# A cross-attention and mixture-of-experts block on one core: ScalarE's exp ahead of its v copies, LN1 one step earlier, the sum over z one step earlier, the high part of z on ScalarE

## The reference

```
q = layernorm(x) @ Wq.T;  k = ctx @ Wk.T;  v = ctx @ Wv.T      # 16 heads of 8
scores = (q . k) / sqrt(8), causal
x = x + (softmax(scores) @ v) @ Wo.T
z = layernorm(x)
rw = softmax(z.mean(over the batch's tokens) @ Wr + br)         # 8 experts
the two best, weights renormalised by a softmax over them
h_e = gelu(z @ W1[e] + b1[e]);  out = sum of the two: w_e * (h_e @ W2[e] + b2[e])
y = out + z;  x = x + layernorm(y) * gamma + beta
```

## Time and profile before

| what | value |
|---|---|
| time, median of 3 runs | 625.79 us (624.58 to 625.92) |
| the profiled execution | 625.34 us, span 623.6 us |
| TensorE matmul, busy share of the span | 88% |
| TensorE weight loads | 62% |
| VectorE | 84% |
| ScalarE | 78% |
| GpSimd | 75% |
| granted TensorE clock, mean | 0.976 |

### The profile page before, as it was taken

The page is one execution under the profiler, slowest core; times in us unless marked ns, Lnnn a source line. Parts: engine busy times, 40 slices in busy tenths (PEclk is TensorE's granted clock), DMA queues, the critical chain, the costliest instruction groups (busy, mean ns, idle before and its releaser), DMA issues.

```text
span 623.6 us, 18950 instructions
## 1 busy us (share of the span) xinstructions
PE 550.3 (88%) x4481; PEld 385.7 (62%) x4481; DVE 521.8 (84%) x1473; ACT 485.9 (78%) x1124; POOL 464.7 (75%) x815
## 2 busy tenths in 40 slices
PE   3899999999999999999999716999999999999782
PEld 2455655556556556555565514788888788888662
DVE  2889898898989898989989756888888888898676
ACT  3677888888787878888887725988888888898494
POOL 5788999999999999999999754755555655554355
PEclk9999999999999999999999967999999999999998
DMA  3010100010010101000020002123322332222135
GB/s 103 27 35 11 35 25 20 22 32 27 8 34 25 34 8 34 25 24 18 17 76 2 2 1 75 56 59 89 98 63 63 89 93 59 85 73 64 44 101 169
DMA packets 55585, 30.03 MB, mean 48 GB/s; under 512 B 4857, under 2 KB 54529, under 8 KB 55553
## 3 DMA queue, kind: packets, MB, share of 16 engines
q1 hardware_dynamic: 55120, 29.47, 16.0%
q10 hardware_dynamic: 432, 0.20, 0.1%
HBM read 13.00 MB, written 4.19 MB: 28 GB/s over the span
## 4 chain that ended last, share of the span: by engine, by line
PE 56%; ACT 14%; DVE 12%; issue 11%; POOL 2%; DVEq 2%; ACTq 2%; DMA 0%; POOLq 0%
PE bank_pair L365 6%; PE scores_banks L354 6%; ACT v_blocks L540 5%; PE scores_banks L484 5%; PE bank_pair L497 5%; PE scores_banks L486 5%; PE scores_banks L485 5%; PE bank_pair L499 5%; PE bank_pair L498 5%; PE bank_pair L378 4%; ACT probs L591 3%; PE bank L328 2%; ACT xn L564 2%; DVE gelu L953 2%; PE bank L390 2%
## 5 line engine op out<-in xcount | busy, mean ns | idle before, releaser
L1072 POOL TENSOR_TENSOR probs<-probs,row_sum_recip 128x512 f32<-128x512 f32 x128 | 133.7, 1045 | 14.7 <-DVE row_sum_recip L792 12.5
L591 ACT ACTIVATE probs<-scores_shifted 128x512 f32<-128x512 f32 x128 | 80.8, 631 | 51.3 <-DVE scores_shifted L786 49.9
L683 ACT ACTIVATE gelu<-scores_banks,b_expert 128x512 f32<-128x512 f32 x144 | 98.5, 690 | 26.3 <-PE scores_banks L486 19.5
L1121 POOL CAST gathered<-z_hi_lo (+1 forms) x114 | 45.9, 438 | 88.7 <-PE scores_banks L486 78.6
L779 DVE TENSOR_REDUCE row_sum<-probs 128x8 f32<-128x512 f32 x128 | 87.1, 680 | 28.7 <-ACT probs L591 28.7
L776 DVE TENSOR_REDUCE row_max<-scores_banks 128x8 f32<-128x512 f32 x128 | 86.9, 679 | 9.1 <-PE scores_banks L354 8.4
L354 PE MATMUL scores_banks<-k_by_head,qT 32*64 32x256 f32 x1024 | 85.0, 401 | 10.3 <-POOL k_by_head L1040 10.2
L902 DVE SCALAR_TENSOR_TENSOR zT_then_yT<-bank_pair,slot_weight,zT_then_yT x288 | 74.7, 282 | 16.9 <-issue 15.5
L786 DVE TENSOR_TENSOR scores_shifted<-scores_banks,row_max 128x512 f32<-128x512 f32 x128 | 86.6, 677 | 0.0
L600 ACT ACTIVATE probsT<-bank_pair 128x512 f32<-128x512 f32 x128 | 76.0, 594 | 13.4 <-PE bank_pair L365 12.6
L365 PE MATMUL bank_pair<-ident,probs 128*128 128x128 f32 x512 | 83.9, 286 | 0.3 <-POOL probs L1072 0.2
(11 more groups left out here) (168 smaller groups left out, 1162.6 us busy)
## 6 DMA issues: line engine op xcount, KB each, us to landing
gathered<-z_hi_lo SPq DMA_DIRECT2D x187, 64.0 KB, 1.8
x_res<-in_x SPq DMA_DIRECT2D x16, 256.0 KB, 2.7
ctxT_pair<-in_ctxT SPq DMA_DIRECT2D x32, 128.0 KB, 2.0
w_raw<-in_w SPq DMA_DIRECT2D x16, 256.0 KB, 3.1
out<-gelu SPq DMA_DIRECT2D x16, 256.0 KB, 2.3
gathered<-z_hi_lo ACTq DMA_DIRECT2D x3, 64.0 KB, 1.9
wq<-in_wq SPq DMA_DIRECT2D x1, 64.0 KB, 2.4
wk<-in_wk SPq DMA_DIRECT2D x1, 64.0 KB, 2.3
```

Source lines behind the costliest of these rows:

```text
L591: nc.scalar.activation(PP[:, (u - 1) % 4, :], SS[:, (u - 1) % 2, :], ACT.Exp, scale=SCALE).then_inc(a_exp, 1)
L683: nc.scalar.activation(G[:, c, :], bank[c][:, :], ACT.Gelu, bias=b1e).then_inc(a_g if c == 0 else a_gp, 1)
L1072: nc.gpsimd.tensor_tensor(pp, pp, RC[:, k % 2, :].unsqueeze(2).to_broadcast([128, 8, S]), ALU.mult).then_inc(g_norm, 1)
```

## The change

Four moves, all in the attention stage:

- ScalarE: in step 0 the exp stands ahead of the v copies instead of behind them.
- LN1 is one step further ahead. ScalarE's two activations (`norm1`) stand in step 2 instead of step 3, GpSimd's reciprocal root in step 0 instead of step 1, and VectorE's statistics, still in step 0, are those of the pair three groups on instead of two; the table of means and variances gets a second buffer, and x is loaded two groups earlier (the second load has 8 tiles instead of 4). VectorE's last pass of its loop over `i` is written out behind it, for the last groups differ.
- VectorE: the sum over z stands in step 2 instead of step 3.
- The high part of z, a cast on GpSimd in step 3, becomes a copy on ScalarE at the end of step 3.

```diff
             # SP
-            sp.dma_start(X[:, 4:8, :], xv[:, 4:8, :]).then_inc(d_x, 16)
+            sp.dma_start(X[:, 4:12, :], xv[:, 4:12, :]).then_inc(d_x, 16)
...
             # ScalarE
+            def keep_z_hi(P):
+
+                act.wait_ge(a_zt, P + 1)
+                nc.scalar.activation(Z2[:, bass.ds(4 * P, 4), 0, :],
+                                     YT[:, bass.ds(256 * P, 256)].rearrange("p (b q) -> p b q", q=S),
+                                     ACT.Copy).then_inc(a_zh, 1)
...
-                    if s == 0 and (not static or 1 <= P < NP):
-                        prep_v(P, h)
                     if not static or 0 <= U - 1 < NB:
                         act.wait_ge(v_sub, U)
                         ge(act, p_t, U - 4)
                         nc.scalar.activation(PP[:, (u - 1) % 4, :], SS[:, (u - 1) % 2, :], ACT.Exp,
                                              scale=SCALE).then_inc(a_exp, 1)
+                    if s == 0 and (not static or 1 <= P < NP):
+                        prep_v(P, h)
...
-                    if s == 3 and (not static or P + 2 < NP):
+                    if s == 2 and (not static or P + 2 < NP):
                         norm1(P + 2)
...
+                    if s == 3 and (not static or 0 <= P - 3 < NP):
+                        keep_z_hi(P - 3)
...
             # VectorE
-                    if s == 0 and (not static or P + 2 < NP):
-                        dve.wait_ge(d_x, 16 * i + 32)
-                        stats1(P + 2)
-                    if s == 3 and (not static or 0 <= P - 3 < NP):
+                    if s == 0 and (not static or P + 3 < NP):
+                        dve.wait_ge(d_x, 16 * i + 16 * h + 16 if not static else max(16 * i + 16 * h + 16, 32))
+                        stats1(P + 3, 1 - h)
+                    if s == 2 and (not static or 0 <= P - 3 < NP):
                         zsum(P - 3)
...
-            stats1(1)
+            stats1(1, 1)
+            dve.wait_ge(d_x, 32)
+            stats1(2, 0)
...
             # GpSimd
-                nc.gpsimd.tensor_copy(hi, z).then_inc(g_zh, 1)
-                pool.wait_ge(g_zh, P + 1)
+                pool.wait_ge(a_zh, P + 1)
                 nc.gpsimd.tensor_tensor(lo, z, hi, ALU.subtract).then_inc(g_zl, 1)
...
-                    if s == 1 and (not static or P + 2 < NP):
-                        rstd1(P + 2)
+                    if s == 0 and (not static or P + 2 < NP):
+                        rstd1(P + 2, h)
```

More of the change, by code:

```diff
@@ L99, in build @@
         ST1 = sb("ln1_stats", [128, 2, 6])
-        MV1 = sb("ln1_mv", [128, 2, 2])
+        MV1 = sb("ln1_mv", [128, 2, 2, 2])
         RS1 = sb("ln1_rstd", [128, 2])
@@ L204, in build @@
                                   sem("v_b1_expert"))
-        v_wl, g_zh, g_zl = sem("v_weights_lo_part"), sem("g_z_hi"), sem("g_z_lo")
+        v_wl, a_zh, g_zl = sem("v_weights_lo_part"), sem("a_z_hi"), sem("g_z_lo")
         p_h, a_g, a_gp, v_gh, v_gl, g_gl, p_l2, v_c = (sem("p_hidden"), sem("a_gelu"), sem("a_gelu_part"),
@@ L258, in _ @@
             sp.wait_ge(d_x, 16)
-            sp.dma_start(X[:, 4:8, :], xv[:, 4:8, :]).then_inc(d_x, 16)
+            sp.dma_start(X[:, 4:12, :], xv[:, 4:12, :]).then_inc(d_x, 16)
             sp.wait_ge(g_const, 3)
             sp.dma_start(B2A[0:E, :], b2).then_inc(d_late, 16)
-            with sp.Fori(1, NP // 2 - 1) as i:
+            with sp.Fori(1, NP // 2 - 2) as i:
                 sp.wait_ge(d_x, 16 * i + 16)
-                sp.dma_start(X[:, bass.ds(i * 4 + 4, 4), :], xv[:, bass.ds(i * 4 + 4, 4), :]).then_inc(d_x, 16)
+                sp.dma_start(X[:, bass.ds(i * 4 + 8, 4), :], xv[:, bass.ds(i * 4 + 8, 4), :]).then_inc(d_x, 16)
                 for par in range(2):
@@ L269, in _ @@
                     sp.dma_start(CT[:, par, :], ctxT[:, bass.ds(i * 512 + par * 256, 256)]).then_inc(d_ct[par], 16)
-            for par in range(2):
-                sp.wait_ge(p_v, NP - 3 + par)
-                sp.dma_start(CT[:, par, :], ctxT[:, 256 * (NP - 2 + par):256 * (NP - 1 + par)]).then_inc(d_ct[par], 16)
+            for P in range(NP - 4, NP):
+                sp.wait_ge(p_v, P - 1)
+                sp.dma_start(CT[:, P % 2, :], ctxT[:, 256 * P:256 * P + 256]).then_inc(d_ct[P % 2], 16)
             for e in range(2):
@@ L634, in _ @@
             keep_z(NP - 1)
+            keep_z_hi(NP - 1)
             def split_hi(loads, par):
@@ L719, in link, with stats1 @@
                 dve.wait_ge(v_chain, chain[0])
-            def stats1(P):
+            def stats1(P, par):
                 n = 2 * P + 2
-                if not isinstance(P, int):
+                if isinstance(P, int):
+                    ge(dve, v_mv1, 2 * P)
+                else:
                     dve.wait_ge(v_max, n)
                 settle(dve, v_setup)
-                ge(dve, g_sh1, P)
+                ge(dve, g_sh1, P - 1)
                 for k in range(2):
@@ L733, in stats1 @@
                 for k in range(2):
-                    nc.vector.bn_aggr(MV1[:, k, :], ST1[:, k, :]).then_inc(v_mv1, 1)
+                    nc.vector.bn_aggr(MV1[:, par, k, :], ST1[:, k, :]).then_inc(v_mv1, 1)
             def residual(T):
@@ L803, in _ @@
             dve.wait_ge(d_x, 16)
-            stats1(0)
+            stats1(0, 0)
             dve.nop().then_inc(v_setup, 1)
@@ L812, in _ @@
             nc.vector.tensor_scalar(WOZ[:, 1, :], WO[:, :], r2mask[:, 1:2], None, ALU.mult).then_inc(v_setup, 1)
-            stats1(1)
+            stats1(1, 1)
+            dve.wait_ge(d_x, 32)
+            stats1(2, 0)
             steps(0)
             steps(1)
-            with dve.Fori(2, NB // 8 - 1) as i:
+            with dve.Fori(2, NB // 8 - 2) as i:
                 steps(i)
+            steps(NB // 8 - 2)
             steps(NB // 8 - 1)
@@ L1023, in rstd, with rstd1 @@
                 nc.gpsimd.tensor_tensor(sh, sh, rs, ALU.mult).then_inc(sh_sem, 1)
-            def rstd1(P):
+            def rstd1(P, par):
                 pool.wait_ge(v_mv1, 2 * P + 2)
                 ge(pool, a_xn, P)
-                rstd(P, MV1[:, :, :], RS1[:, :], SH1[:, :], g_eps1, g_rs1, g_sh1)
+                rstd(P, MV1[:, par, :, :], RS1[:, :], SH1[:, :], g_eps1, g_rs1, g_sh1)
             def rstd2(P, h):
@@ L1079, in steps @@
                         split_z(P - 3)
-            rstd1(0)
+            rstd1(0, 0)
             causal_mask()
@@ L1084, in _ @@
             spread_k(0, 0, range(4))
-            rstd1(1)
+            rstd1(1, 1)
             pool.wait_ge(d_late, 96)
```

## The result

The changed kernel takes 617.13 us (median of 4 runs, 616.13 to 618.10) against 625.48 in the same runs: a ratio of 0.9862, 95% interval 0.984 to 0.9883, so 8.4 us faster. The forecast was faster by 4.2, a time of 621.5: the sign and the mechanism held, the gain is twice the size. The profiled execution is the fastest of the four, 616.13.

A forecast was written before the change was run, and what follows sets the result against it. A once-a-group loop of waits, not one engine, was taken as the bound at 10.69 us; six terms gave 10.53, so 309.92 became 304.1, with ends +0.79 and +0.76: 4.2 us faster, 621.5 us, range 617 to 626.

The forecast's parts named there:

- new loop: Exp, v copies, projection, TensorE to step 2's scores, row max, VectorE to step 3's subtract, exp; 10.53 us per group.
- term 6: VectorE from step 2's row max to step 3's subtract: 3.49 plus 0.39 for the z sum, 3.88 us.
- term 2: ScalarE from exp to first v copy: 0.60 us, the middle of 0.54 and 0.65.
- term 3: From the first v copy to TensorE's projection, which waits for the fourth: 1.30 us.
- term 4: TensorE from projection to turn of z, 2.27, and on to step 2's scores, 0.99: together 3.26 us.
- term 5: From scores on TensorE to a VectorE row max that waits for them: 0.78 us.
- the ends of the stage: Attention stage's first and last groups: start +0.79, last period +0.76, first two groups after the start about 9.9 us each.
- The slower rival: ScalarE's high-part copy holds up step 0's exp: loop 10.81, about 629 us; chance 0.10.
- The rival "much faster": TensorE paces nothing and can catch up, leaving VectorE alone at 9.79 a group: about 599 us; chance 0.07.
- The rival "nothing gained": Second path, ScalarE's k/xn copy to step 1's q matmul, 0.08 shorter; might restore 10.69, 625 to 626 us; chance 0.15.
- worth nothing by itself: Moving LN1's activations, statistics and root touches nothing on the new loop, so it gains zero alone.
- old loop: Step 0 exp, row sum, residual, turn of z, TensorE to step 3, probability copy, LN1's pair, v copies, exp; 10.69 us.

The follow-up runs named there:

- zsum_twice: The changed kernel with the z sum of step 2 done twice, the second into a tile that nothing reads: 626.74 us, period 10.72.
- hi_after_exp: The changed kernel with ScalarE's copy of the high part of z moved to the next group's step 0, between exp and v copies: 625.57 us.
- zsum_back: The changed kernel with the sum over z back in step 3: 611.75 us, period 10.21.
- hi_alone: The kernel before with only the high part of z moved, from GpSimd's cast to a ScalarE copy at the end of step 3: 634.79 us.
- hi_on_pool: The changed kernel with the high part of z as a GpSimd cast in step 3 again, ScalarE's copy gone: 617.50 us.
- ln1_alone: The kernel before with only LN1 one step forward, its loads included: 614.05 us, ratio to before 0.9799.
- exp_alone: The kernel before with only the step 0 exp moved ahead of the v copies: 618.50 us, ratio to before 0.9892.
- v_first_hi_early: The changed kernel with v copies ahead of the exp, z sum in step 3, ScalarE's high-part copy in step 2 ahead of the probability copy: 605.58 us.

## Why the prediction was right and wrong

**Right: the mechanism.** The v copies and the projection close a new loop, and it is the pace. Shown three ways: its corners add up to the period; work added to it costs one to one at two of its places (zsum_twice, hi_after_exp); work taken from it gains until the next path comes (zsum_back). The projection's wait of 0.5 and the row maxima's waits were forecast, VectorE's wait for the exp is gone, and so is the k spreading's hold on step 0's scores. One sign did not come. GpSimd was to have half a microsecond more idle time; its busy time falls by 0.39 (9.92 to 9.53), but the period falls by as much, and it stands idle for 0.82 of a group against 0.84.

**The step that failed: the sum of the new loop, 10.53, was mis-sized by 0.14 a group.** Term by term against the rows after:

- the z sum in term 6: 0.39 forecast, 0.29 measured (3.78 against 3.88 for the stretch). It is 0.36 long; the forecast took a whole duration (0.38 in the earlier trace rows). In a run of instructions what counts is the distance to the next start: 215.99 to 216.28.
- term 2, exp to v copies: 0.60 taken, the middle of 0.54 and 0.65; 0.53 measured. The v copies behave like the q copy.
- the rest: 0.71 as forecast, term 3 1.29 for 1.30, term 4 3.24 for 3.26, term 5 0.80 for 0.78.

Together 0.18 less, so 10.35; 0.04 of it is lost again on the mean, where ScalarE's loop over `i` turns, for which the sum has no term (the periods before alternate too, 10.65 and 10.76): 10.39. Over 27 groups 0.14 is 3.8 us, nearly all of the 4.2 that were missing. The old period stood at 10.69 and the new floor near it, so an error of 1.4% in the floor doubled the gain. The time lies just inside the stated range, 617 to 626, and outside the forecast's own, 618.5 to 624.5, which allowed for both ends of term 2 and for the ends of the stage but took the z sum as certain. That the wider range still holds it is luck.

A page bears on the first point. The Trainium skill (Perfetto Trace Analysis, Optimizing Scalar/DVE Operations) says that an instruction's data access in SBUF costs some 60 ns on VectorE and 93 on ScalarE, and that its profiled latency shows about twice that, since the half for the write's acknowledgement overlaps with the next instruction. The rows agree in kind: 0.36 long and 0.29 to the next start on VectorE, 0.41 and 0.30 on ScalarE (hi_alone).

**The other parts.** *High part by ScalarE*: nothing in this change, as forecast (hi_on_pool). The slower rival did not come: the copy took 0.417, and ScalarE still waited 0.28 for the subtract behind it. (GpSimd keeps a wait in the place of the cast, now for ScalarE's copy, and was not held up by it.) *Loads*: the doubled load landed 5.3 us after its issue, and the first row max, at 13.81 against 13.98 in the earlier trace rows, still waited for the scores and not for the load: hidden. *The rival "much faster"*: TensorE waits for the v copies and holds up the scores, though its weight loads fill only 6.08 of 10.35. The Trainium skill's rule that the forecast names (Perfetto Trace Analysis, Identifying the Most-Contended Engine) judges one engine, and here a loop through three engines sets the pace. *The rival "nothing gained"*: the q matmul did not wait.

**LN1 one step forward, "worth nothing by itself", was wrong outside the change.** The pair stood in the old loop, as the forecast's own reading of it says, and without it that loop is 0.77 shorter. ln1_alone shows it: 614.05. What it gives inside the change no run shows, since the change without it was not run. exp_alone speaks against "nothing": there the exp has moved, the pair still stands in step 3, and TensorE waits 0.5 a group for the attention copy behind it, at a period of 10.41. So of the four parts one (LN1) is enough, one (the z sum) costs some 5 us where it was put, one (the exp) costs 6 to 7 in the company of v_first_hi_early, and one (the high part) is free in the change and worth 8.5 where GpSimd is the floor.

The ends came out near the forecast: start +0.73 (0.79), last period +0.58 (0.76), the two groups after the start 19.27 (2 x 9.9). For the start that is partly luck. hi_on_pool has the same instructions up to there, and its second v copies stand at 24.76, where the change has them at 23.23: its scores at 16.89 still take 1.13, those of the change at 16.01 take 0.66, while the granted clock reads 1.00 there in both.

ln1_alone is 3 us faster than the change at the same settled period, and the two profiles show where. The last v copies stand at 333.37 in the change and at 330.60 in ln1_alone, 2.77 apart. Of that 1.46 is there at the second v copies (23.23 and 21.77): before, they stood at 22.50, and the exp ahead of them costs the change 0.73, while ln1_alone gains 0.73 without LN1's pair ahead of them. Another 0.58 comes in the last period (10.35 and 9.77), and 0.73 in between, where some of ln1_alone's first groups take only 9.77 to 9.88 before GpSimd becomes the pace.

What stays open: what the change would be without LN1's move, and which path paces v_first_hi_early (9.88 and 10.18 in turn).

## What to carry to other kernels

When all engines are nearly full and none is, write out the loop of waits, and the loop that the change closes, and compare their lengths. Size their terms by the distance from one start to the next, not by durations, and where the two loops are within a few per cent of each other give the gain a range as wide as that difference. Before several moves are judged together, ask of each which loop it stands in: a move that relieves what is not the floor has no effect until another move makes it the floor (the high part of z), and work moved from a pause into the loop costs up to its whole distance to the next start.

## What the runs showed of the hardware that was not expected

- The same copy of 128x256 on ScalarE was free at the end of step 3 and cost 0.30 us a group one instruction later, between the exp and the v copies; its row shows 0.42 in the first place and 0.40 in the second.
- A doubled load took twice as long to land: 512 KB in 5.3 us against 2.7 for 256 KB.

```profile
x_res<-in_x SPq DMA_DIRECT2D x14, 256.0 KB, 2.7
x_res<-in_x SPq DMA_DIRECT2D x1, 512.0 KB, 5.3
```
